# Three of four last shared-expert groups moved in front of the first row transposes

## What is computed

```python
    logits = xf @ Wg
    _, topi = jax.lax.top_k(logits, K)              # K = 2 of E = 16 experts
    gates = jax.nn.softmax(jnp.where(mask, logits, -jnp.inf), axis=-1)
    for e in range(E):
        h = jax.nn.silu(xf @ W1[e] + b1[e]) * (xf @ W11[e] + b11[e])
        y = y + (h @ W2[e] + b2[e]) * gates[:, e, None]
    z = jax.nn.silu(xf @ Ws1 + bs1) * (xf @ Ws11 + bs11) @ Ws2 + bs2
    x = x + jnp.tanh(g_ffn[0]) * (y + z)
```

## Time and profile before

| | us |
|---|---|
| median of three runs | 588.08 |
| lowest and highest of them | 586.46, 592.04 |
| time of the profiled execution | 588.39 |
| its span in the trace | 586.2 |
| TensorE matmul busy | 552.7 (94%) |
| VectorE busy | 362.7 (62%) |
| ScalarE busy | 226.8 (39%) |
| GpSimd busy | 337.0 (57%) |

### The profile page before, as it was taken

One profiled execution on the slowest core, in us unless ns is written; L12 is line 12 of the kernel. 1 busy time (PEld: TensorE's weight loads), 2 busy tenths in 40 slices (PEclk: granted clock), 3 DMA queues, 4 the chain that ended last, 5 costly groups with the idle time before them and its releaser, 6 DMA issues.

```text
span 586.2 us, 11866 instructions
## 1 busy us (share of the span) xinstructions
PE 552.7 (94%) x3212; PEld 442.3 (75%) x3213; DVE 362.7 (62%) x860; ACT 226.8 (39%) x760; POOL 337.0 (57%) x278
## 2 busy tenths in 40 slices
PE   5789999999987999988999999999999999999995
PEld 4456666666656888867888888888888888888884
DVE  5559788888765662225655566655556665345685
ACT  1687887777786211111221222222122222233231
POOL 5577799899885255670455655364444650246660
PEclk9799999999998999989999999999999999999999
DMA  7662100000020235244257868558556210022324
GB/s 260 273 233 88 29 28 21 25 27 34 12 82 19 91 94 211 82 153 173 75 194 248 286 239 292 184 188 290 199 181 237 89 45 28 29 63 81 90 73 144
DMA packets 32321, 76.07 MB, mean 130 GB/s; under 512 B 4896, under 2 KB 21408, under 8 KB 29344
## 3 DMA queue, kind: packets, MB, share of 16 engines
q1 hardware_dynamic: 12944, 51.52, 24.7%
q10 hardware_dynamic: 16272, 15.74, 8.5%
q0 software_dynamic: 3072, 8.39, 4.5%
HBM read 54.93 MB, written 18.61 MB: 125 GB/s over the span
## 4 chain that ended last, share of the span: by engine, by line
PE 72%; POOL 13%; issue 8%; DVE 3%; ACT 2%; DMA 1%; POOLq 1%; ACTq 0%; DVEq 0%
PE mid L673 14%; PE big L654 7%; PE big L656 7%; PE big L655 7%; POOL arena L1346 5%; PE big L573 5%; PE big L574 5%; PE big L575 5%; PE mid L664 4%; POOL arena L1332 3%; PE work L426 2%; PE last L592 2%; PE work L638 2%; PE work L592 2%; PE big L455 1%
## 5 line engine op out<-in xcount | busy, mean ns | idle before, releaser
L827 ACT ACTIVATE last<-arena 128x512 f32<-128x512 f32 x47 | 28.3, 602 | 184.0 <-DVE arena L1228 184.0
L757 ACT ACTIVATE arena<-big,nmax 128x128 f32<-128x128 f32 x256 | 90.0, 387 | 11.8 <-DVE nmax L943 11.8
L673 PE MATMUL mid<-dring,arena 128*128 x376 | 88.9, 379 | 0.0
L1228 DVE TENSOR_TENSOR arena<-big,bring 128x512 f32<-128x512 f32 x47 | 32.5, 692 | 87.7 <-PE big L656 87.7
L654 PE MATMUL big<-u_hi,xsT_hi 128*128 x188 | 82.4, 438 | 0.8 <-issue 0.8
L1346 POOL TENSOR_TENSOR arena<-arena,rinv 128x1024 f32<-128x1024 f32 x32 | 60.7, 1896 | 25.3 <-DVE rinv L951 25.3
L1362 POOL TENSOR_TENSOR u_lo<-arena,u_hi 128x2048 fp32r<-128x2048 f32 x16 | 73.4, 4585 | 1.3
L656 PE MATMUL big<-u_hi,xsT_lo 128*128 x188 | 73.8, 392 | 0.0
L673 PEld LDWEIGHTS mid<-dring,arena 128*128 128x128 f32 x376 | 67.9, 190 | 7.3
L655 PE MATMUL big<-u_lo,xsT_hi 128*128 x188 | 73.2, 390 | 0.0
L1440 POOL TENSOR_TENSOR pool_mark<-mhalf 128x1 f32<-128x1 f32 x15 | 2.9, 193 | 101.8 <-PE big L656 84.8
(11 more groups left out here) (162 smaller groups left out, 1165.1 us busy)
## 6 DMA issues: line engine op xcount, KB each, us to landing
arena<-up_w_dram SPq DMA_DIRECT2D x16, 1024.0 KB, 7.6
bring<-expert_bias_dram SPq DMA_DIRECT2D x16, 640.0 KB, 5.3
dring<-down_w_dram SPq DMA_DIRECT2D x18, 512.0 KB, 3.4
sorted_y<-arena ACTq DMA_DIRECT2D x47, 128.0 KB, 1.8
arena<-sorted_x ACTq DMA_DIRECT2D x43, 128.0 KB, 2.1
sorted_x<-dring SPq DMA_DIRECT2D x3, 1536.0 KB, 8.4
dring<-up_w_dram SPq DMA_DIRECT2D x2, 1024.0 KB, 4.9
xf_all<-xfs SPq DMA_DIRECT2D x16, 128.0 KB, 2.0
```

Of the source, the lines that this page charges most:

```text
L673: i = mm(mid[:, 1, 0:D], gT[:, p, c, :], dring[:, slot, c * D:(c + 1) * D], start=(c == 0), stop=(c == HC - 1))
L757: i = nc.scalar.activation(probs[:, u % 2, h, :], big[:, u % 2, h // 4, (h % 4) * CTX:(h % 4 + 1) * CTX], ACT.Exp, bias=nmax[:, u % 2, h:h ...
```

## The change

On TensorE three of the four groups of step 3 come before the first row transposes, where one stood between the first two transposes and three behind the first `up`. One group stays behind the first `up`. A wait for `z_taken` >= 14 is added in front of the first transposes, since they write the bank `work`, which group 13 has used. On VectorE the takes of the groups are moved to match. Nothing is added to or taken from the work.

```diff
+            shared_down(3, range(3))
+            pe.wait_ge(z_taken, 3 * GROUP + 2)
             transpose_rows(0, 0)
-            shared_down(3, range(1))
             transpose_rows(1, 1)
             up(0, 0)
             pe.wait_ge(xsT_ready, 2)
-            shared_down(3, range(1, GROUP))
+            shared_down(3, range(3, GROUP))
             pe.wait_ge(z_taken, 4 * GROUP)
             transpose_rows(2, 2)
             up(1, 1)
...
             add_shared(2)
+            add_shared(3, range(3))
             copy_rows(0, 0)
-            add_shared(3, range(1))
             copy_rows(1, 1)
...
             add_biases(0, 0)
-            add_shared(3, range(1, GROUP))
+            add_shared(3, range(3, GROUP))
             copy_rows(2, 0)
```

## The result

| | median us | runs | ratio to the kernel before | 95% interval |
|---|---|---|---|---|
| before, beside the first set | 589.43 | 20 | | |
| changed, first set | 591.51 | 20 | 1.0046 | 1.0024 to 1.0068 |
| before, beside the second set | 590.11 | 35 | | |
| changed, second set | 590.18 | 12 | 1.0000 | 0.9974 to 1.0025 |
| before, beside the third set | 590.02 | 32 | | |

A forecast was written before the change was run, and what follows sets the result against it. TensorE was taken as the bound, with 72% of the chain. Its path from 257.11 to up(1) was summed to 14.86 us against 16.52, a gain of 1.66: 588.39 - 1.66 = 586.7 us, range 585.0 to 589.4.

The forecast's parts named there:

- The start of the path, 257.11: End of step 2's last group on TensorE, 255.38 + 1.73, where the next group could start.
- With the clock staying up: Condition of the main forecast of 586.7 us: TensorE's granted clock does not fall in the changed stretch; chance 0.45.
- Rival 1: Clock falls once, over two gaps round block 1's transposes, costing 1.1 to 1.7: 587.8 to 588.4 us; chance 0.34.
- The gap between the transposes: From block 0's transposes to block 1's, which wait for VectorE's row copies: 1.71 us, about 1.3 of it idle.
- The reading of the expert: Register reading between block 1's transposes and up(0): 1.29 us from the transposes' start to the first matmul.
- The slow first group and the second reading: Group 12 was priced at 1.73 us, and block 2's transposes with the reading ahead of up(1) at 1.29.
- About 1.3 of it is clock that is no longer lost: Share of the 1.66 us gain: 1.14 from group 12 at full clock, the rest in the transposes.
- the covered wait for the rows: Block 0's rows, there at 260.04, come 2.3 us before its transposes can start at 262.30.
- the even pace of the three groups: Three groups straight behind step 2's take 3 x 1.73 = 5.19 us.
- Rival 2: Clock falls twice, again over up(1), costing 1.7 us more: 590.1 us; chance 0.07.
- Rival 3: TensorE's reading of the expert stays hidden under its waits, 1.15 us better: 585.6 us; chance 0.07.
- rival 4: Gain is lost later, where GpSimd or a weight load comes to rule a block: 588.4 us; chance 0.04.

The follow-up runs named there:

- e6: Changed kernel without the older wait for z_taken 12: ratio 0.9975 to the kernel before, 18.49 us from group 11 to up(1).
- e2: Changed kernel with five idle matmuls added in the gaps round block 1's transposes: ratio 0.9985 to the kernel before, 18.03 us from group 11 to up(1).
- e7: Changed kernel with the experts of blocks 0 and 1 read ahead of the three groups, older wait kept: ratio 0.9990 to the kernel before.
- e10: Changed kernel without the older wait for z_taken 12 and with both experts read ahead of the three groups: ratio 0.9938 to the kernel before.
- e1: Changed kernel run again without edit, the second set: ratio 1.0000 to the kernel before, 19.66 us from group 11 to up(1).
- e11: Kernel before with four idle matmuls put into its wait for the rows of block 0: ratio 0.9976, 17.94 us from group 11 to up(1).
- e9: Changed kernel run a third time without edit, the third set: ratio 1.0004 to the kernel before, 19.50 us from group 11 to up(1).
- e8: Changed kernel, groups placed 2, 1 and 1, two in their own bank, older wait gone, both experts read ahead: ratio 0.9845 to the kernel before.
- e5: Kernel before run again without edit, as control: ratio 0.9992, 18.76 us from group 11 to up(1).
- e3: Changed kernel with two groups before the first transposes, one between the first two, one behind the first up: ratio 0.9991 to the kernel before.

## Why the prediction was wrong, step by step

**The start of the path, 257.11: wrong, 0.96.** "The order of work is the same up to 257.11" was right, but "where the next group could start" was not. The older wait for `z_taken` 12 stands in the code between group 11 and what follows. In the trace before it could not be seen, since it ended under the wait for the rows. I priced the wait that the change adds and missed the one that it uncovers. e6 shows it.

**"With the clock staying up": wrong, 1.6.** Rival 1 came true: 2.15 us of forecast idle time were 2.6 in the trace, the clock fell in all four profiles with the pair of gaps, and the 1.59 that it cost `up(0)` lies in the rival's 1.1 to 1.7. e2 takes the fall away with idle matmuls and gets 1.63 back. I gave the forecast 0.45 and this rival 0.34, though the nearest row pointed to the fall. The Trainium skill, "TensorE: Matmul & The Clock Gate", section "A second HAM failure mode: psum-queue depth-cycling", says that short pauses between groups of matmuls can take the clock down and up again. It spoke for the rival, and the traces agree with it here, with 1.44 and 1.15.

**The gap between the transposes: right in kind, 0.11 too small** (1.71 against 1.82). **The reading of the expert: right in kind, 0.25 too small** (1.29 against 1.54). e7 and e10 show that it is the reading: with it done ahead, 0.68 is left. **The slow first group and the second reading** add 0.07 and 0.15, and group 15 with its take came out 0.06 shorter.

The sum for e1: 16.59 + 0.96 + 1.59 + 0.11 + 0.25 + 0.07 + 0.15 - 0.06 = 19.66, the distance that was measured. Against 18.25 and 18.76 before, that is 0.9 to 1.4 us more. The mean of the three ratios (1.0018, 1.1 us) is near it, but since the sets hardly overlap this agreement may be luck.

**"About 1.3 of it is clock that is no longer lost": too large.** e11 gives 0.3 to 0.8, since the slow group had hidden the reading. The sentence behind it doesn't add up either: 2.77 of idle time less 1.3 and 0.85 would leave 0.62, where the sum of 1.66 leaves 0.36.

**Right were** the covered wait for the rows, the even pace of the three groups, that the added wait costs nothing, that `up(0)` waits for block 1's transposes and its reading, and that all behind `up(1)` is only shifted. Rival 2 did not come: the clock was back by the second pair of gaps in each of these profiles. Rival 3 did not come, nor rival 4.

**The base and what stays open.** The measured 591.51 is 4.8 above the forecast of 586.7: 1.04 is the base (589.43 against 588.39), 1.66 the gain that did not come, and 2.08 the difference of the two medians. The first set (1.0046, 2.7 us) is 1.3 to 1.8 above what the path explains; the other two are about 1 below it, which their intervals allow. The one profile of the first set shows late takes: TensorE waited 0.50 for VectorE at 247.79, among step 3's up matmuls, and 0.96 ahead of group 11, 1.5 together. The mean clocks of the runs fit this in part. At a mean granted clock of 0.991 to 0.993 ten runs of the first set span 587.0 to 591.8, while the three runs of e1 and e9 at 0.991 span 585.5 to 586.0. Those runs of the first set were longer at the same clock, as they would be by more waiting; but at 0.989 four of the first set span 587.3 to 590.8 and six of e1 and e9 589.2 to 589.9, which is no difference. And one profile doesn't show that all 20 runs had late takes, and e1's profile, which has none, took 591.18 against 591.32. What made the takes late was not found; the code up to there is that of the kernel before, and none of the profiles of the twelve experiments shows such a take. e1 and e9 ran on two different chips, and which one the first set had is not known, so a cause in the chip is open too.

## What to carry to other kernels

A wait for data can hide other waits in the code behind and before it. Before you fill it with moved work, list every wait on that engine from the last instruction ahead of it to the first behind it, and price each as if it stood bare. A move that empties the queue between two small instructions exposes what the queue had covered (a reading of registers, a copy on another engine), and a pair of such gaps can bring TensorE's clock down on the work behind them. Spread the work that can move so that each gap gets some: with the older wait gone and both experts read ahead, the same four groups made 0.9938 when placed 3 and 1 (e10), and 0.9845 when placed 2, 1 and 1 with a bank of their own (e8). Without these cures 3 and 1 made 1.00.

## What the runs showed of the hardware that was not expected

Idle matmuls can pay: five of them, 2.2 us of extra matmul time in gaps of the same length, shortened the path by 1.63 (e1 to e2), and the clock stayed at 1.00 where it had fallen.

A register read from a table (`item_of`) is no small thing on TensorE when it stands bare: two of them ahead of group 12 made it 1.57 later (4.26 in e7 against 2.69 in e1), and one ahead of `up(0)` 0.86 (1.54 against 0.68).

The kernel before scatters with the clock. In the 29 beside e5 to e8 the three with a mean granted clock of 0.995 span 584.0 to 584.4, and the 17 at 0.989 span 587.6 to 589.4. Part of its scatter of 6 us thus goes with the clock. The profiles show where: the stretch behind `up(1)` is the same in all fourteen to 0.6 us, while group 11 starts anywhere from 253.40 to 258.74, behind code that no version changes. It starts earliest in e3 and e11 (253.40 and 253.51), the only two in which the clock did not fall between 20 and 30 us; in the others it starts at 255.02 or later. A change of 1 us has to be told from that.
